# Two transformer layers on one core: each norm of the first three groups split between VectorE and ScalarE, large loads issued later, all engine orders rewritten

## The reference

```python
x = _layernorm(x + _L0_attn_ref(x, ...))   # a gated linear recurrence over time, 16 heads of 8 x 8 state
x = _layernorm(x + _L0_ffn_ref(x, ...))    # x @ W[idx] + b[idx]; idx is the argmax of noisy logits over 8 experts
x = _layernorm(x + _L1_attn_ref(x, ...))   # linear attention without a softmax, with a metric per head
x = _layernorm(x + _L1_ffn_ref(x, ...))    # silu(x w1) * (x w2), two hidden 512 x 512 layers with gelu, then w3
```

## Time and profile before

| what | us |
|---|---|
| runs of the kernel before | 199.05, 200.31, 201.71 (median 200.31) |
| the profiled execution | 198.95 |
| its span in the trace | 197.2 |
| PE busy in the span | 178.5 (91%) |
| DVE busy | 143.8 (73%) |
| ACT busy | 124.7 (63%) |
| POOL busy | 63.9 (32%) |

### The profile page before, as it was taken

How to read it: one execution, slowest core, us unless ns; L and a number is a source line. 1 busy time by engine, 2 the same in 40 slices (tenths; PEclk the granted TensorE clock), 3 DMA queues, 4 the chain that set the end, 5 groups by cost and what they waited for, 6 DMA issues and landing times.

```text
span 197.2 us, 2885 instructions
## 1 busy us (share of the span) xinstructions
PE 178.5 (91%) x949; PEld 140.4 (71%) x949; DVE 143.8 (73%) x375; ACT 124.7 (63%) x207; POOL 63.9 (32%) x61
## 2 busy tenths in 40 slices
PE   7797999698799999999999999999999999899940
PEld 7454685385697687997789889987678886576830
DVE  0699999989799999499779991777860545803572
ACT  3879972845304797635884663467877569885630
POOL 0020001420001152843504234490516572465511
PEclk9999999998899999999999999999999999999997
DMA  4998000210000000100000000000000100001102
GB/s 118 243 421 366 3 2 22 76 38 3 0 0 0 2 3 0 49 8 0 0 0 2 3 0 0 0 0 0 3 2 0 53 5 0 0 6 48 53 3 57
DMA packets 6704, 7.83 MB, mean 40 GB/s; under 512 B 544, under 2 KB 5664, under 8 KB 6432
## 3 DMA queue, kind: packets, MB, share of 16 engines
q1 hardware_dynamic: 6688, 7.63, 11.7%
HBM read 6.58 MB, written 1.05 MB: 39 GB/s over the span
## 4 chain that ended last, share of the span: by engine, by line
PE 56%; issue 15%; DVE 9%; ACT 9%; DMA 3%; POOL 3%; SPq 2%; POOLq 0%; DVEq 0%; ACTq 0%
PE c_bank L1386 33%; PE y_bank L1291 6%; PE b_bank L1320 6%; DMA xt<-x_tok 3%; ACT normed_lent L417 3%; PE b_bank L1347 2%; DVE state L832 2%; PE b_bank L1315 2%; SPq L239 1%; POOL res L293 1%; DVE stats L875 1%; PE b_bank L1386 1%; DVE read L842 1%; ACT gate L528 1%; PE sum_bank L1386 1%
## 5 line engine op out<-in xcount | busy, mean ns | idle before, releaser
L832 DVE TENSOR_TENSOR_SCAN state<-rep_bank,keep 128x256 f32<-128x256 f32 x62 | 38.8, 673 | 0.3 <-PE rep_bank L1278 0.3
L305 POOL TENSOR_TENSOR rstd<-varied,power 128x4 f32<-128x4 f32 x15 | 15.2, 1010 | 62.5 <-DVE varied L889 62.5
L1291 PEld LDWEIGHTS y_bank<-attend_pack,read 128*128 128x128 f32 x256 | 31.5, 192 | 5.0 <-DVE read L842 2.6
L1291 PE MATMUL y_bank<-attend_pack,read 128*128 128x128 f32 x256 | 33.1, 277 | 0.5 <-DVE read L842 0.3
L842 DVE TENSOR_TENSOR read<-state,query 128x512 f32<-128x512 f32 x32 | 22.4, 707 | 0.1
L314 POOL TENSOR_TENSOR hid_odd_low<-hid,hid_odd_high 128x512 fp32r<-128x512 f32 x12 | 15.7, 1311 | 20.2 <-ACT hid L545 20.1
L545 ACT ACTIVATE hid<-c_bank,scales_pack 128x512 f32<-128x512 f32 x31 | 21.0, 682 | 0.0
L1386 PE MATMUL c_bank<-hid_even_high,hidden_rounded 128*128 128x512 f32 x64 | 19.4, 414 | 0.5 <-ACT gate L528 0.5
L1386 PE MATMUL c_bank<-hid_odd_low,hidden_rounded 128*128 128x512 f32 x64 | 18.6, 400 | 0.5 <-DVE hid_odd_low L985 0.5
L1386 PE MATMUL c_bank<-hid_odd_high,hidden_rounded 128*128 128x512 f32 x64 | 18.7, 404 | 0.2 <-ACT hid L545 0.2
L539 ACT ACTIVATE hid_even_high<-c_bank,scales_pack 128x512 fp32r<-128x512 f32 x15 | 10.3, 688 | 13.2 <-PE c_bank L1386 13.1
(11 more groups left out here) (188 smaller groups left out, 361.7 us busy)
## 6 DMA issues: line engine op xcount, KB each, us to landing
hidden_pack<-hidden SPq DMA_DIRECT2D x2, 1024.0 KB, 10.5
xt<-x_tok SPq DMA_DIRECT2D x4, 256.0 KB, 2.8
xT_lent<-x_chan SPq DMA_DIRECT2D x3, 256.0 KB, 5.9
mlp_pack<-mlp SPq DMA_DIRECT2D x1, 768.0 KB, 7.7
out<-xT_lent SPq DMA_DIRECT2D x3, 256.0 KB, 2.3
attend_pack<-attend SPq DMA_DIRECT2D x1, 640.0 KB, 4.2
metric_pack<-metric SPq DMA_DIRECT2D x1, 448.0 KB, 11.8
xT_lent<-x_chan SPq DMA_DIRECT2D x2, 128.0 KB, 2.5
```

The source lines that it names most:

```text
L305: nc.gpsimd.tensor_tensor(rstd[n][:], varied[n][:], power[:], ALU.pow).then_inc(ln_rstd[n], 1)
L832: ins = nc.vector.tensor_tensor_scan(state[:, e % STATES, at], rep_bank[e % 2][:, at], keep[:, a * T + s * SEQ:a * T + (s + 1) * SEQ], 0.0 ...
L1291: ins = nc.tensor.matmul(y1_bank[:, tile(j)], read[:, e % READS, tile(j)], out_w_rep_sb[:, e, :], start=(e == 0 and j == 0), stop=False, s ...
```

## The change

Three parts, in the words of the code.

1. **Shared norms.** A table says that ScalarE writes 2 of the 4 tiles for norms 0, 1, 2 of groups 0, 1, 2; VectorE writes the other 2. Each half has its own semaphore, and whoever waits for a tile waits for the semaphore of its writer. For groups 0 and 1 this moves two tiles from ScalarE to VectorE; for group 2 it moves two from VectorE to ScalarE and adds a `norm_shift`. Group 3 and norm 3 stay as they were.
2. **Loads.** The tokens of group 0 are loaded before x of groups 2 and 3, SyncE then waits until x of group 1 has landed, and the metric pack is issued ahead of the three MLP packs.
3. **Orders.** The lists of VectorE, ScalarE, TensorE and GpSimd are written anew. The casts of the MLP weights move behind norm 0 of group 0; `passed_weights` and the second `attend_residual` move ahead of the first `inverse_std`; `top_remainder` moves up on VectorE and `flag_sum` on TensorE.

```diff
+ACT_TILES = {(0, 0): 2, (0, 1): 2, (0, 2): 2, (1, 0): 2, (1, 1): 2, (1, 2): 2, (2, 0): 2, (2, 1): 2, (2, 2): 2}
...
+        def vector_tiles(n, g):
+            return NT - ACT_TILES.get((n, g), 0)
...
+        def wait_tile(engine, n, g, j):
+
+            if j < vector_tiles(n, g):
+                engine.wait_ge(ln_out[n], vector_total(n, g - 1) + j + 1)
+            else:
+                done = sum(NT - vector_tiles(n, i) for i in range(g))
+                engine.wait_ge(ln_out_act[n], done + j - vector_tiles(n, g) + 1)
...
-            load_tokens(0)
-            for pack in ("mlp", "hidden1", "hidden2", "metric"):
+                if g == 1:
+                    load_tokens(0)
+
+                    sp.wait_ge(xT_loaded[1], 16)
+            for pack in ("metric", "mlp", "hidden1", "hidden2"):
                 load_pack(pack)
...
             attend_residual(0)
+            passed_weights()
+            attend_residual(1)
             inverse_std(0, 0)
-            attend_residual(1)
-            passed_weights()
...
-                for j in range(NT):
+                for j in range(vector_tiles(n, g), NT):
                     nc.scalar.activation(normed[n][:, tile(j)], total[n][:, tile(j)], ACT.Identity,
-                                         bias=shift[n][:, j:j + 1], scale=rstd[n][:, j:j + 1]).then_inc(ln_out[n], 1)
+                                         bias=shift[n][:, j:j + 1], scale=rstd[n][:, j:j + 1]).then_inc(ln_out_act[n], 1)
...
-                for j in range(NT):
+                for j in range(vector_tiles(n, g)):
                     nc.vector.tensor_scalar(normed[n][:, tile(j)], total[n][:, tile(j)], moments[n][:, j, 0:1],
                                             rstd[n][:, j:j + 1], ALU.subtract, ALU.mult).then_inc(ln_out[n], 1)
...
-                    pe.wait_ge(ln_out[n], NT * b + j + 1)
+                    wait_tile(pe, n, b, j)
```

More of the change, by code:

```diff
@@ L218, in build @@
         ln_shift = [sem(f"ln{n}_shift") for n in range(3)]
+        ln_out_act = [sem(f"ln{n}_out_act") for n in range(3)]
         centred = sem("centred")
@@ L709, in _ @@
             whole_gelu(2, 2, 3)
+            high_x3(3)
             silu(3, 0)
@@ L1035, in _ @@
             norm_shift(0, 0)
+            norm_out(0, 0)
+            direct_product(1)
+            low_values(2, 0)
             scan(1, 3)
-            scan(1, 4)
-            read_state(1, 2)
-            low_values(2, 0)
+            read_state(1, 0)
             norm_sum(1, 0)
-            read_state(1, 3)
+            read_state(1, 1)
             norm_stats(1, 0)
             norm_moments(1, 0)
+            read_state(1, 2)
+            norm_varied(1, 0)
+            read_state(1, 3)
+            scan(1, 4)
@@ L1099, in _ @@
             scan(3, 0)
+            low_values(3, 1)
+            scan(3, 1)
+            scan(3, 2)
+            mask_gram(1)
             read_state(2, 7)
-            mask_gram(1)
+            scan(3, 3)
             direct_product(3)
-            scan(3, 1)
-            read_state(3, 0)
+            low_gelu(0, 1, 3)
             norm_sum(0, 2)
@@ L1107, in _ @@
             norm_stats(0, 2)
-            read_state(3, 1)
+            norm_moments(0, 2)
+            norm_varied(0, 2)
             norm_sum(2, 1)
-            low_gelu(0, 1, 3)
             norm_stats(2, 1)
@@ L1113, in _ @@
             norm_varied(2, 1)
-            norm_moments(0, 2)
-            low_values(3, 1)
-            norm_varied(0, 2)
             norm_shift(2, 1)
-            scan(3, 2)
-            scan(3, 3)
-            low_x3(1)
+            norm_out(2, 1)
+            read_state(3, 0)
+            norm_shift(0, 2)
             norm_out(0, 2)
@@ L1596, in with_weights @@
                 attend(2, 4)
-                attend(2, 5)
                 sum_query(3)
-                replicate(2, 7)
                 hidden(0, 1, 0)
                 hidden(0, 1, 1)
+                replicate(2, 7)
+                attend(2, 5)
+                replicate(3, 0)
                 transposes(1, 1)
-                replicate(3, 0)
+                hidden(0, 1, 2)
+                heads_of(1)
+                replicate(3, 1)
+                replicate(3, 2)
+                hidden(0, 1, 3)
```

402 lines of the change are left out of this document (205 added, 197 removed).

## The result

| | before | after |
|---|---|---|
| median of 14 runs each, us | 199.07 | 202.50 |
| lowest and highest | 197.95, 201.71 | 201.41, 203.93 |
| the profiled execution, its span | 198.95, 197.2 | 201.85, 200.0 |
| ratio after to before | | 1.0175, 95% interval 1.0142 to 1.0208 |

The kernel became slower by 3.4 us. The forecast was 0.7 us faster. The time lies inside the forecast's range (195.4 to 202.6), just under its upper end, and on the other side of no change. The forecast had started from 200.31, the median of three runs; over 14 runs the kernel before stands at 199.07.

A forecast was written before the change was run, and what follows sets the result against it. VectorE was taken to bound the kernel up to 80 us, TensorE after; +1.7 - 2.4 + 0.5 + 0.3 - 0.2 - 0.5 = -0.6, called -0.7, gave 199.6 us from 200.31, range 195.4 to 202.6.

The forecast's parts named there:

- The bound: Up to 80 us VectorE is full and TensorE follows it; from 80 us on TensorE sets the end.
- Work added on VectorE: Before norm 1 of group 1: four more two-tile blocks, 2.28 us, plus 1.25 less 1.84 behind the shift: +1.7 us.
- point of reckoning: Last tile of norm 1 of group 1, near the end of VectorE's stage, written at 77.88 us before the change.
- Idle time taken away: VectorE's early waits for the gram mask (1.4), norm 1's sum (0.7) and a scan (0.3) all go: -2.4 us.
- New waits: On VectorE, 0.4 us at the routing's first step and 0.1 at `top_remainder`: +0.5 us.
- order on TensorE: By the point of reckoning TensorE has one more `replicate` behind it, 0.23 us of work: -0.2 us.
- VectorE beside GpSimd: Of five two-tile blocks on VectorE perhaps half of one meets a GpSimd subtraction: +0.3 us, between 0 and 5.5.
- Norm 2 of group 1: After 80 us, ScalarE's part of this norm is half as long and stands one gelu later: -0.5 us.
- Group 2 and later: Group 2's norms cost nothing as VectorE has idle time; later orders nearly the same, last chain keeps its steps: 0.
- C: Other waits replace VectorE's three early ones, so no idle time goes away: 202.0 us, chance 0.15.
- B: The flag sum comes late for `top_remainder` and VectorE stands for it: 202.7 us, chance 0.13.
- A: TensorE bounds the first stage; passed_w's wait, low clock (1.7 us), tile waits and norm 2 give 5.5 us: 194.8, chance 0.22.

The follow-up runs named there:

- e6_sum_late: Changed kernel with the metric pack loaded ahead of x of groups 2 and 3 and ScalarE's first low-halves sum two projections later: 198.09 us, ratio 0.9964 to the old kernel.
- e2_metric_first: Changed kernel with only the metric pack loaded ahead of x of groups 2 and 3, TensorE's metric step staying early: 200.13 us, ratio 1.0055 to the old kernel.
- e7_tiles_first: `e6_sum_late` with VectorE's shift and two tiles of group 2's norm 2 ahead of group 3's norm 0 sum and statistics: 197.75 us, ratio 0.9947 to the old kernel.

## Why the prediction was wrong, step by step

*The bound.* Right. With the two waits removed VectorE is busy 24.41 of 25 us and then 9.9 of 10 (`e6_sum_late`), and after 80 us TensorE is full: 15.00 of 15 and 35.00 of 35 in the changed kernel.

*Work added on VectorE, +1.7.* Right. The four blocks, at 37.01, 46.42, 61.59 and 66.43 us, took 0.60 each (forecast 0.57; the instruction behind one starts 0.51 after it), and the fifth, behind the shift, too:

```profile
79.69 0.60 DVE L940 TENSOR_SCALAR normed_lent<-normed_lent,moments,rstd 128x128 f32<-128x128 f32 x2
```

This is also the point of reckoning: the last tile of norm 1 of group 1 is written at 80.29 us, 2.4 us later than the 77.88 of before, where the sum's terms on VectorE (+1.7 - 2.4 + 0.5 + 0.3) had it 0.1 later. In `e6_sum_late` the same block starts at 75.54 and ends at 76.14. What lies between VectorE's first scan and this norm's shift, before, after and in `e6_sum_late`:

```profile
8.49:75.87 67.38, 59.86 (x334) 44.84 (x335) 64.14 (x152) 43.11 (x71) 10.99 (x10) 0.97 0.20 73
7.96:78.78 70.82, 59.26 (x331) 44.71 (x332) 66.27 (x161) 38.74 (x61) 11.65 (x10) 0.95 0.20 70
7.88:74.63 66.75, 58.14 (x331) 43.74 (x332) 65.86 (x160) 38.63 (x61) 11.95 (x10) 0.97 0.21 75
```

VectorE's busy time (the third of the five) grew by 2.1 us, a little less than the sum had it (2.28, and 0.3 for GpSimd). Its idle time, the rest of the stretch, grew from 3.2 to 4.6 us, by 1.3, where the sum had it shrink by 1.9 (-2.4 + 0.5). This is the error, and it is all in the waits.

*Idle time taken away, -2.4.* Right for 2.1 of it: the waits for the gram and for norm 1's sum are gone. The scan's wait of 0.3 was to go with x of group 1 landing earlier. That x did land earlier (TensorE's first step on it starts at 9.47 us, before 10.28), but VectorE reached the scan earlier too, and stood 0.5.

*New waits, +0.5.* This is the step that failed. The two that I named came to 0.2 us (`top_remainder`) and nothing (the routing's first step started at 15.26 without a wait). But VectorE's new waits are 3.4 us. What I had not priced were two steps that read a pack: `project_metric`, moved forward on TensorE past the load of its pack, of which the step "order on TensorE" counted nothing but one `replicate`; and `sum_low_halves(0)`, which did not move much but whose pack came 2.8 us after ScalarE wanted it, once ScalarE itself was no longer late (`e2_metric_first`). I had booked the held back loads as a gain for x of group 1 alone and never asked when the held ones would land. That question had rows in the trace of before. Its view of the loads has the metric pack, from issue to landing (the last figure, us):

```profile
metric_pack<-metric SPq DMA_DIRECT2D x1, 448.0 KB, 11.8
```

With up to 11.8 us for a pack that can't be issued before x of group 1 is in, at 9 to 10 us, a step at 13 us that reads it has an upper bound of 9 us of waiting, more than the upper bound of any other term of the sum.

*VectorE beside GpSimd, +0.3.* The size is about right and the place wrong, so this is luck. None of the five blocks met a subtraction. A `read_state`, which the sum did not think of, met one and took 0.9 us more:

```profile
70.08 1.58 DVE L871 TENSOR_TENSOR read<-state,query 128x512 f32<-128x512 f32 x1
...
69.83 2.98 POOL L335 TENSOR_TENSOR hid_even_low<-hid,hid_even_high 128x512 fp32r<-128x512 f32 x2 [3.62 <-ACT hid_even_high L560]
```

(Before, one at 37.28 us took 0.4 more beside GpSimd's residual.) A shared block of two tiles met a subtraction only at 131 us, where the sum had zero.

*Order on TensorE, -0.2.* Too small to be read apart.

*Norm 2 of group 1, -0.5.* Right in kind: the gap of TensorE at 95.6 us is gone. By the rows it was worth 0.24 (PE 35.00 of 35 us, before 34.76).

*Group 2 and later, 0.* Wrong by about 1 us, the wait of 1.03 at 132.37. I had argued with VectorE's idle share, and a mean share says nothing of what stands just ahead of the instruction that TensorE waits for.

*The rivals.* What came is C (202.0): other waits took the place of those removed, and by my own test (VectorE's waits of 2 us or more) C was the case. I had given it 0.15, and looked for the wait among the steps of group 0's chain and not in the loads. B did not come: `top_remainder` waited 0.2. A is not borne out. One of its two dearest parts was TensorE's clock, 1.7 us, and two traces price it. `e6_sum_late` and `e7_tiles_first` have the same lists up to 125 us; one has a stretch at a lower clock and the other has none (10 to 185 us all at 1.00). From 35 to 45 us, `e6_sum_late` first:

```profile
35.00:45.00 10.00, 9.11 (x54) 7.54 (x55) 9.93 (x27) 5.05 (x8) 1.39 (x1) 0.83 0.00 1
35.00:45.00 10.00, 7.95 (x54) 6.66 (x55) 9.93 (x27) 5.09 (x8) 1.38 (x1) 1.00 0.00 1
```

TensorE has 54 matmuls in both and is busy 1.2 us longer with them at the lower clock, out of its idle time; VectorE is busy 9.93 of 10 in both, and reaches the shift of norm 1 of group 1 at 74.63 and 74.67 us. So the low clock cost nothing there, and it comes and goes between executions of the same steps.

With both waits removed the kernel comes out at -0.7 us (ratio 0.9964, with an interval that reaches no change), which is the forecast's figure, but partly by accident. At the point of reckoning its trace is 1.7 us ahead, where the terms had it 0.1 behind. By the three rows above: 0.6 is an earlier first scan (7.88 us, before 8.49), which the sum did not have (VectorE's list now begins with the routing's first steps); the idle time fell by 2.4 and no new wait took 0.5 of that back; the work came to 1.7 in place of 2.28 + 0.3; and the part behind the shift gave 0.5. Later about 1 us was lost at norm 2 of group 2. Nor may the 1.7 be set against the -0.7 to tenths: the profiled execution of `e6_sum_late` took 197.34 us, under its kernel's median of 198.09.

## What to carry to other kernels

- Moving a step forward past other steps can also move it past a load. For each such step write down which load it reads, when that load is issued in the new list and how long it takes to land; do the same for every reader of a load that is held back, on all engines.
- Two waits that stand side by side hide each other: removing one gave 0.2% or 0.6 to 1.2%, removing both 2%. When a cure gives less than expected, look in its trace for the next wait at the same place before giving up the theory.
- A division of work between two engines and the order around it are one decision. The same sharing was worth 2.0% in lists written for it and cost 2.5% in lists that were not.
- The time of a load also decides when the engine behind it works, and so what that work meets. Earlier tokens made GpSimd's residual earlier, and a `read_state` on VectorE then took 1.65 us for 0.68.

## What the runs showed of the hardware

- In these traces the instruction that starts second pays. Two tiles of 0.60 us on VectorE that started 0.04 us behind a subtraction on GpSimd took 1.58, and the subtraction its usual 1.28. Where the tiles started 0.38 us ahead, they took 0.60 and the subtraction 1.37. Four tiles that started 0.31 ahead took 2.21 for 1.11 all the same: each tile is an instruction of its own. GpSimd's inverse root took 1.38 us at 44.16, behind a `read_state` that had started at 43.98, and 1.01 at 59.94 and at 77.74. The rule of the Trainium skill cited in the prediction ("SBUF — State Buffer", "Who interferes with whom": the first one keeps the shared ports for its whole instruction, the other blocks) fits the first case, 0.98 us more of a subtraction's 1.28.
- A `read_state`, a product of two SBUF tiles of 128x512 on VectorE, took 1.58 and 1.65 us for 0.68 when it started 0.25 to 0.38 us behind a subtraction or a residual on GpSimd.
- TensorE stood 2.70 us (after 0.99 and a short matmul), and in its next work its clock was mostly at the lower level, 1.2 GHz of 2.4: 0.58 of full between 15 and 19 us, where a pair of matmuls took 1.92 us for 1.02.
- The activation table's load, 1.28 us, is issued where the list stands and does not wait for what its activation waits for: at 15.37 us it lay wholly in ScalarE's idle time, and behind a waiting instruction of another kind it came at 20.03, on the path.
